# An ALiBi attention stage, rewritten as one pipeline over sequences

## The chip, the cores and the metric

The kernel runs on one core of a Trainium2 chip. The metric is the device time of one execution in microseconds. The profiled execution is one run of the same program, and its times are counted from the first instruction (the span's start).

## What is computed

A decoder of four layers runs over x, eight sequences of 128 positions and 256 features, in float32. Each layer has three sublayers, twelve stages in all. The change is in the first sublayer of the third layer, a causal self-attention with ALiBi (a bias that grows with distance, with a slope for each head), 16 heads of 16 features:

```python
qkv = jnp.einsum('bsd,de->bse', x, W_qkv)
q, k, v = jnp.split(qkv, 3, axis=-1)
q, k, v = (to_heads(q), to_heads(k), to_heads(v))
attn = jnp.einsum('bhqd,bhkd->bhqk', q, k) / math.sqrt(HEAD_DIM)
attn = attn + alibi_bias(seq_len, N_HEADS)[None] + causal_mask(seq_len)[None, None]
attn = jax.nn.softmax(attn, axis=-1)
y = jnp.einsum('bhqk,bhkd->bhqd', attn, v)
y = y.transpose(0, 2, 1, 3).reshape(bsz, seq_len, n_embd)
return jnp.einsum('bsd,de->bse', y, W_o)
...
x = x + _L2_attn_ref(_layernorm(x, axis=-1), L2_attn_W_qkv, L2_attn_W_o)
```

The slope of head h (from 1 to 16) is 2 to the power -8/h.

## The kernel before

Five queues run side by side: TensorE (PE), VectorE (DVE), ScalarE (ACT), GpSimd (POOL) and SyncE (SP), which starts the DMAs. Each runs its own instructions in the order in which they are written, and waits on semaphores for the others. There is no planner. The stages follow each other, and x, all eight sequences, stays in SBUF.

The stage of the change, L2a, is a loop `Fori(0, 4)` on each of the three engines, over pairs of sequences (suffixes 0 and 1, each with half of PSUM, `ps0` and `ps1`). For one sequence:

- VectorE normalises x (`bn_stats`, `bn_aggr`, `tensor_scalar`, L2815 to L2828, and for the next pair L2925 to L2945) with a ScalarE `Ln` and `Exp` for the inverse root. TensorE transposes the result, ScalarE copies it to SBUF (`unT0`, `unT1`).
- TensorE makes q and k, transposed, with eight matmuls (L4084 and L4091), and v with two (L4095, L4099).
- To separate heads of 16 features inside 128 partitions, VectorE multiplies k with the mask `mask16` into eight copies (`kM_0`, `kM_1`, L2832 to L2836, 128x1024 each, two a sequence). A matmul of 128 rows then gives the scores of four heads, 128x512, because seven eighths of k are zeros.
- For each group of four heads (four groups a sequence): VectorE adds the bias head by head out of PSUM, takes the row maxima, and multiplies them by -0.25. ScalarE takes the exponentials head by head, with the maximum as bias. TensorE transposes four 128x128 blocks, ScalarE copies them (`PT_0`), TensorE multiplies with v. v has a 17th column of ones, so that the sum of a row comes out with the product, VectorE takes the reciprocal of four sums and multiplies.
- TensorE transposes the result (`ao_0`), ScalarE copies it, TensorE applies the output weights (L4205, L4220), VectorE adds x (L2947, L2949).

```python
dve.scalar_tensor_tensor(S_0[:, 3, :], alibi[:, :], 1.0, ps0[:, 1, 384:512], ALU.mult, ALU.add)
...
dve.tensor_reduce(st0[:, 16:20], S_0[:, :, :], AX.X, ALU.max).then_inc(L2a_vector_done, 1)
...
dve.tensor_scalar(st0[:, 16:20], st0[:, 16:20], -0.25, None, ALU.mult).then_inc(L2a_vector_done, 1)
...
                for i in range(4):
                    last = act.activation(S_0[:, i, :], S_0[:, i, :], ACT.Exp, scale=0.25, bias=st0[:, 16 + i:17 + i])
```

`alibi` holds key position minus query position, and -1e30 where the key lies ahead of the query. GpSimd does nothing in the stage but one memset for a later stage (L1143), which waits for L2a. SP issues the weights of a later stage (L964 to L982) when L2a's last projection is done.

The stage behind it, L2x, starts with statistics of x (L2959, L2961), a ScalarE table load, and the scaling of its weights.

Two stages further on use shapes that matter here. The last one, L3f, has scores as eight matmuls of 32 rows and 256 columns (L4698, 16 records), outputs as matmuls of 32 weight columns (L4715), maxima and subtractions over 128x1024 (L3375, L3381). The one before it, L3x, takes a reciprocal of 128x256 (L3296).

## Time and profile before

| | us |
|---|---|
| median of 3 runs | 2380.74 (2378.89 to 2381.53) |
| the profiled execution | 2377.16 |
| its span, first to last instruction | 2375.4 |
| TensorE busy | 1984.6 (84%) |
| VectorE busy | 1531.1 (64%) |
| ScalarE busy | 1149.6 (48%) |
| GpSimd busy | 921.4 (39%) |

The busy times are sums over the whole program; which engine holds a stage up must be read from that stage. TensorE's granted clock over the whole span is 0.919 of its full 2.4 GHz. A float32 matmul shows as two records, a transpose as one.

### The profile page before, as it was taken

How to read it: one execution, taken by the hardware profiler on the slowest of the kernel's cores; microseconds unless marked ns; L12 is line 12 of the kernel's file. 1: busy time of each engine (PE TensorE's matmuls, PEld its weight loads, DVE VectorE, ACT ScalarE, POOL GpSimd, SP SyncE). 2: the span in 40 equal slices, each digit the busy share in tenths (PEclk: the TensorE clock that was granted, in tenths of full speed). 3: DMA queues.
4: the chain of work that ended last, by engine and by line, in shares of the span. 5: the costliest groups of instructions: out<-in, count | busy, mean ns of one | idle time of the engine just before them, and what ended most of it. 6: DMA issues, size and time to landing. Idle time of an engine off the chain costs nothing.

```text
span 2375.4 us, 32699 instructions
## 1 busy us (share of the span) xinstructions
PE 1984.6 (84%) x10924; PEld 1460.6 (61%) x10924; DVE 1531.1 (64%) x2892; ACT 1149.6 (48%) x2702; POOL 921.4 (39%) x651
## 2 busy tenths in 40 slices
PE   6677797786899886679999999967888879977999
PEld 5111185344799764467777777756777755544888
DVE  5798824557444575456666666548999967866443
ACT  4444323342232355655555555546666645644443
POOL 2699801210000000144444454439999950002221
PEclk9688897798899897789999999988999988998999
DMA  4111001002000502000000000000000010000000
GB/s 149 38 36 27 0 1 53 18 16 106 18 0 0 213 0 91 0 1 1 1 1 1 1 1 1 1 18 1 1 1 1 25 43 30 1 1 0 6 7 9
DMA packets 20858, 54.66 MB, mean 23 GB/s; under 512 B 8319, under 2 KB 13608, under 8 KB 18424
## 3 DMA queue, kind: packets, MB, share of 16 engines
q1 hardware_dynamic: 20728, 53.01, 6.6%
q8 instruction: 72, 1.18, 0.2%
q14 instruction: 58, 0.48, 0.1%
HBM read 44.61 MB, written 1.05 MB: 19 GB/s over the span
## 4 chain that ended last, share of the span: by engine, by line
PE 48%; DVE 20%; ACT 11%; issue 11%; POOL 9%; SPq 1%; DMA 0%; DVEq 0%; POOLq 0%; ACTq 0%
POOL sbuf L1193 4%; DVE sbuf L2237 3%; PE psum L4309 3%; PE psum L4251 3%; DVE sbuf L3001 2%; PE psum L3551 2%; POOL sbuf L1201 2%; ACT sbuf L1826 2%; PE psum L4299 2%; PE psum L4382 1%; PE psum L4735 1%; PE psum L4756 1%; PE psum L4742 1%; DVE sbuf L2993 1%; PE psum L4255 1%
## 5 line engine op out<-in xcount | busy, mean ns | idle before, releaser
L1193 POOL TENSOR_TENSOR sbuf<-sbuf 128x1035 f32<-128x1035 f32 x128 | 248.4, 1971 | 0.9 <-ACT sbuf L1894 0.9
L4382 PE MATMUL psum<-sbuf 128*128 128x128 f32 (+1 forms) x1024 | 144.4, 292 | 56.0 <-ACT sbuf L1903 39.6
L1903 ACT ACTIVATE sbuf<-sbuf 128x1001 f32<-128x1001 f32 (+1 forms) x128 | 141.6, 1139 | 97.9 <-DVE sbuf L3144 63.6
L4382 PEld LDWEIGHTS psum<-sbuf 128*128 128x128 f32 (+1 forms) x1024 | 126.3, 153 | 77.5 <-ACT sbuf L1903 55.9
L1155 POOL TENSOR_TENSOR sbuf<-sbuf 128x512 f32<-128x512 f32 x64 | 69.7, 1090 | 230.9 <-DVE sbuf L3018 230.9
L1082 POOL TENSOR_TENSOR sbuf<-sbuf 128x1024 f32<-128x1024 f32 x64 | 149.9, 2356 | 15.6 <-DVE sbuf L2237 14.9
L2237 DVE TENSOR_TENSOR_SCAN sbuf<-psum,sbuf 128x1024 f32<-128x1024 f32 x64 | 144.6, 2277 | 13.6 <-ACT psum L1314 6.9
L3499 PE MATMUL psum<-sbuf 96*128 96x512 bf16 x256 | 84.0, 439 | 75.1 <-DVE sbuf L2237 32.3
L4251 PE MATMUL psum<-sbuf 128*128 128x512 f32 x256 | 124.1, 608 | 17.4 <-DVE sbuf L2980 17.4
L3136 DVE SCALAR_TENSOR_TENSOR psum<-sbuf,psum 128x1024 f32<-128x1024 f32 (+1 forms) x96 | 122.3, 1274 | 12.8 <-PE psum L4372 5.4
L4309 PE MATMUL psum<-sbuf 128*128 128x256 f32 x512 | 125.5, 389 | 4.9 <-POOL sbuf L1163 4.9
L1314 ACT ACTIVATE psum<-psum,sbuf 128x1016 f32<-128x1016 f32 x64 | 68.9, 1081 | 125.1 <-PE psum L3499 125.1
L1826 ACT ACTIVATE sbuf<-psum,sbuf 128x128 f32<-128x128 f32 x256 | 90.6, 366 | 77.3 <-DVE sbuf L3012 77.3
L3144 DVE TENSOR_TENSOR sbuf<-psum,sbuf 128x1024 f32<-128x1024 f32 (+1 forms) x96 | 116.4, 1212 | 3.3
L1143 POOL MEMSET sbuf<- 128x720 f32 x1 | 0.7, 700 | 302.9 <-PE psum L4106 302.9
L3499 PEld LDWEIGHTS psum<-sbuf 96*128 96x128 bf16 x256 | 19.0, 104 | 152.8 <-DVE sbuf L2237 60.3
L4309 PEld LDWEIGHTS psum<-sbuf 128*128 128x128 f32 x512 | 99.6, 195 | 20.2 <-POOL sbuf L1163 6.1
L4299 PE MATMUL psum<-sbuf 128*128 128x256 f32 x256 | 73.3, 409 | 39.8 <-ACT sbuf L1833 39.8
L1161 POOL TENSOR_TENSOR sbuf<-sbuf 128x512 f32<-128x512 bf16 x64 | 74.4, 1162 | 68.6 <-DVE sbuf L3031 66.4
L3001 DVE TENSOR_REDUCE sbuf<-sbuf 128x6 f32<-128x768 f32 x64 | 60.8, 949 | 52.2 <-ACT sbuf L1796 52.2
L1163 POOL TENSOR_TENSOR sbuf<-sbuf 128x512 f32<-128x512 f32 x64 | 81.4, 1272 | 5.0
L3530 PE MATMUL psum<-sbuf 128*32 128x512 f32 x256 | 78.9, 748 | 3.5 <-POOL sbuf L1082 3.5
(1073 smaller groups left out, 5253.9 us busy)
## 6 DMA issues: line engine op xcount, KB each, us to landing
sbuf<-sbuf SPq DMA_DIRECT2D x42, 128.0 KB, 2.4
sbuf<-w_gu_d SPq DMA_DIRECT2D x1, 4096.0 KB, 13.6
sbuf<-w_p_d SPq DMA_DIRECT2D x1, 4096.0 KB, 25.3
sbuf<-w_qkv_d SPq DMA_DIRECT2D x3, 768.0 KB, 4.2
sbuf<-w_e_d SPq DMA_DIRECT2D x1, 2048.0 KB, 7.5
sbuf<-w_dn_d SPq DMA_DIRECT2D x1, 2048.0 KB, 16.6
sbuf<-w_q_d SPq DMA_DIRECT2D x1, 2048.0 KB, 7.4
sbuf<-w_qx_d SPq DMA_DIRECT2D x1, 2048.0 KB, 11.9
```

What stands on the lines that cost most here:

```text
L1082: pool.tensor_tensor(L0a_hc[i % 4][:, :], L0a_hs[i % 2][:, :], L0a_Cr[g % 4][:, :], ALU.mult).then_inc(hc_done, 1)
L1193: pool.tensor_tensor(P_r[g % 7][:, :, :], rows.unsqueeze(2).to_broadcast([128, 23, 45]), cols.unsqueeze(1).to_broadcast([128, 23, 45]), AL ...
L1826: last = act.activation(prob[:, h, :], L2x_s[:, h, :], ACT.Exp, bias=smax[:, h:h + 1], accum_out=esum[:, h:h + 1])
L1903: act.activation(Q_r[g % 6][:, 0:w], Q_r[g % 6][:, 0:w], ACT.Silu, scale=q8_p[n % 2][:, h:h + 1]).then_inc(silu_done, 1)
L2237: dve.tensor_tensor_scan(L0a_hs[i % 2][:, :], L0a_dAf[i % 2][:, :], L0a_us[i % 3][:, :], 0.0, ALU.mult, ALU.add).then_inc(scan_done, 1)
L3001: dve.tensor_reduce(ssum[:, :], sq[:, :, :], AX.X, ALU.add).then_inc(ss_done, 1)
L3136: dve.scalar_tensor_tensor(M[:, 0:w], Pf_r[g % 7][:, o:o + w], t8_p[n % 2][:, h, 7:8], zps[:, 0:w], ALU.is_ge, ALU.mult).then_inc(mask_don ...
L3144: dve.tensor_tensor(Q_r[g % 6][:, 0:w], Mps[:, 0:w], Pf_r[g % 7][:, o:o + w], ALU.mult).then_inc(prod_done, 1)
L4251: last = pe.matmul(L2x_q[:, :, :], xs[:, vq, c, :], wq[:, c, 512 * g:512 * g + 512], start=c == 0, stop=c == 1)
L4299: last = pe.matmul(L2x_o[:, 2 * h:2 * h + 2, :], v2_r[i % 3][:, h, :], pT2[:, 2 * h:2 * h + 2, :], start=True, stop=True)
L4309: last = pe.matmul(L2x_out[:, :], cat[:, h, :], w_p2[:, 4 * (i % 8) + h, :], start=i % 8 == 0 and h == 0, stop=i % 8 == 7 and h == 3)
L4382: last = pe.matmul(Gps[0:m, c, :], Q_r[g % 6][:, 128 * c:128 * c + m], ident[:, :], start=h == 0 and c % 4 == 0, stop=h == 7, skip_group_c ...
```

## The change

The three `Fori` loops of L2a are replaced by one pipeline over the eight sequences, written out, with its own small functions and the semaphores of the neighbouring stages.

- Scores: k is expanded by a mask of two (`L2a_mask2`) instead of eight, 128x512 a sequence. Four matmuls of 32 rows each, at partitions 0, 32, 64 and 96, take two heads each, twice: eight matmuls of 256 columns for all 16 heads.
- Bias: GpSimd fills a table of all slopes times `alibi`, -1e30 included, 16 blocks of 128x128, early in the kernel. VectorE adds it to the scores in two operations of 128x1024 (`L2a_bias`).
- Softmax: VectorE takes the maxima over 128x1024 and subtracts them itself (`L2a_sub`); ScalarE takes two exponentials of 128x1024 without bias.
- Outputs come transposed, with v as 32 weight columns (16 of them zeros); 16 more matmuls with `L2a_ones` give the row sums, repeated over the features, 128x256. VectorE takes the reciprocal of all 128x256 and multiplies. No transpose of the result is needed.
- GpSimd normalises x. The statistics of all sequences are taken at the stage's start.
- The waits of SP, of GpSimd's memset and of the next stage go to the new semaphores, and the starting numbers of later stages' semaphores change with them.

```diff
+            for a in range(2):
+                for h in range(8):
+                    head = h // 2 % 2 * 8 + 4 * a + h // 4 * 2 + h % 2
+                    last = pool.tensor_scalar(L2a_table[:, a, h, :], alibi[:, :], 4.0 * 2.0 ** (-8.0 / (head + 1)), None, ALU.mult)
+            last.then_inc(factor_done, 1)
...
+                pool.tensor_scalar(L2a_u[:, :], x[:, n, :], L2a_mv[:, n, 0:1], L2a_r[:, n:n + 1], ALU.subtract, ALU.mult).then_inc(u_done, 1)
...
+            def L2a_exp(n, a):
+                act.wait_ge(sub_done, L2a_start['sub'] + 2 * n + a + 1)
+                act.activation(L2a_P[a][:, :, :], L2a_P[a][:, :, :], ACT.Exp, scale=0.25).then_inc(exp_done, 1)
+
+            def L2a_pTc(n, a):
+                act.wait_ge(pT_done, L2a_start['pT'] + 2 * n + a + 1)
+                if n > 0:
+                    act.wait_ge(o_done, L2a_start['o'] + n)
+                act.activation(L2a_PT[a][:, :, :], L2a_pT[:, :, :], ACT.Copy).then_inc(pTc_done, 1)
...
+            for i in range(9):
+                if i > 0:
+                    L2a_pTc(i - 1, 1)
+                if i < 7:
+                    L2a_qTc(i + 1)
+                if i < 8:
+                    L2a_exp(i, 0)
+                if i < 7:
+                    L2a_vc(i + 1)
+                if i < 8:
+                    L2a_pTc(i, 0)
+                    L2a_exp(i, 1)
+                if i < 6:
+                    L2a_unTc(i + 2)
...
+            def L2a_keys(n):
+                dve.wait_ge(qTc_done, L2a_start['qTc'] + n + 1)
+                if n > 0:
+                    dve.wait_ge(score_done, L2a_start['score'] + n)
+                dve.tensor_tensor(L2a_kM[:, :, :, :], L2a_front[:, 256:512].rearrange('p (c s) -> p c s', c=2).unsqueeze(2).to_broadcast([128, 2, 2, 128]), L2a_mask2[:, None, :].unsqueeze(3).to_broadcast([128, 2, 2, 128]), ALU.mult).then_inc(kTc_done, 1)
+
+            def L2a_bias(n, a):
+                dve.wait_ge(score_done, L2a_start['score'] + n + 1)
+                if n > 0:
+                    dve.wait_ge(pT_done, L2a_start['pT'] + 2 * n + a - 1)
+                dve.tensor_tensor(L2a_P[a][:, :, :], L2a_S8[a][:, :, :], L2a_table[:, a, :, :], ALU.add).then_inc(prod_done, 1)
...
+                dve.tensor_reduce(L2a_mx[a][:, :], L2a_P[a][:, :, :], AX.X, ALU.max).then_inc(max_done, 1)
...
+                dve.tensor_tensor(L2a_P[a][:, :, :], L2a_P[a][:, :, :], L2a_mx[a][:, :].unsqueeze(2).to_broadcast([128, 8, 128]), ALU.subtract).then_inc(sub_done, 1)
+
+            def L2a_scale(n):
+                dve.wait_ge(o_done, L2a_start['o'] + n + 1)
+                dve.reciprocal(L2a_rec[:, :, :], L2a_sums[:, :, :]).then_inc(recip_done, 1)
+                dve.wait_ge(recip_done, L2a_start['recip'] + n + 1)
+                if n > 0:
+                    dve.wait_ge(proj_done, L2a_start['proj'] + n)
+                dve.tensor_tensor(L2a_aoT[:, :, :], L2a_oT[:, :, :], L2a_rec[:, :, :], ALU.mult).then_inc(norm_done, 1)
+
+            def L2a_resid(n):
+                dve.wait_ge(proj_done, L2a_start['proj'] + n + 1)
+                dve.tensor_tensor(x[:, n, :], L2a_out[:, :], x[:, n, :], ALU.add).then_inc(resid_done, 1)
...
+            for i in range(9):
+                if i < 8:
+                    L2a_bias(i, 0)
+                    L2a_max(i, 0)
+                    L2a_sub(i, 0)
+                    L2a_bias(i, 1)
+                if i < 7:
+                    L2a_keys(i + 1)
+                if i < 8:
+                    L2a_max(i, 1)
+                    L2a_sub(i, 1)
+                if i > 0:
+                    L2a_scale(i - 1)
+                    L2a_resid(i - 1)
...
+            def L2a_scores(n):
+                pe.wait_ge(kTc_done, L2a_start['kTc'] + n + 1)
+                if n > 0:
+                    pe.wait_ge(prod_done, L2a_start['prod'] + 2 * n)
+                for c in range(2):
+                    for r in range(4):
+                        last = pe.matmul(L2a_S[:, r, c, :, :], L2a_qT[32 * r:32 * r + 32, c, :], L2a_kM[32 * r:32 * r + 32, c, :, :], start=True, stop=True)
+                last.then_inc(score_done, 1)
...
+                            pe.matmul(L2a_oT[32 * r:32 * r + 32, c, :], L2a_v[n % 2][:, 4 * c + r, 32 * e:32 * e + 32], L2a_PT[r // 2][:, 4 * (r % 2) + 2 * c + e, :], start=e == 0, stop=e == 1)
...
+                            last = pe.matmul(L2a_sums[32 * r:32 * r + 32, c, :], L2a_ones[:, 32 * e:32 * e + 32], L2a_PT[r // 2][:, 4 * (r % 2) + 2 * c + e, :], start=e == 0, stop=e == 1)
+                last.then_inc(o_done, 1)
+
+            def L2a_project(n):
+                pe.wait_ge(norm_done, L2a_start['norm'] + n + 1)
+                for c in range(2):
+                    last = pe.matmul(L2a_out[:, :], L2a_aoT[:, c, :], w_o2[:, c, :], start=c == 0, stop=c == 1)
+                last.then_inc(proj_done, 1)
...
+            for i in range(9):
+                if i < 8:
+                    L2a_scores(i)
+                if i > 0:
+                    L2a_pTr(i - 1, 1)
+                if i < 7:
+                    L2a_qk(i + 1)
+                if i > 0:
+                    L2a_pv(i - 1)
+                if i < 7:
+                    L2a_value(i + 1)
+                if i < 8:
+                    L2a_pTr(i, 0)
+                if i < 6:
+                    L2a_uTr(i + 2)
+                if i > 0:
+                    L2a_project(i - 1)
```

Not shown are `L2a_uTr`, `L2a_qk`, `L2a_value` (the same matmuls as before, one sequence at a time), `L2a_pTr` (eight transposes), `L2a_unTc`, `L2a_qTc`, `L2a_vc` (ScalarE's copies), the statistics, and the memsets for v and ones.

## Rows read from the trace of the kernel before

**Rows 1.** Busy time by engine: the stage, and one loop pass (two sequences).

```profile
core 0: us, PE busy (x) PEld busy (x) DVE busy (x) ACT busy (x) POOL busy (x), PEclk, DMA share, GB/s
788.37:932.68 144.31, 126.87 (x676) 94.86 (x676) 93.24 (x312) 73.98 (x214) 0.70 (x1) 0.88 0.17 72
861.70:896.00 34.30, 30.83 (x168) 22.84 (x168) 22.84 (x76) 18.15 (x52) 0.00 (x0) 0.90 0.00 0
```

**Rows 2.** Timeline at the stage's end: start, us, engine, line, idle before.

```profile
932.26 0.42 DVE L2949 TENSOR_TENSOR sbuf<-psum,sbuf 128x256 f32 x1 [2.33 <-PE psum L4220]
932.76 1.28 ACT L1835 ACT_TABLE_LOAD   x1
932.78 0.42 DVE L2959 BATCH_NORM_STATS2 sbuf<-sbuf 128x6 f32<-128x256 f32 x1
933.24 0.18 DVE L2961 BATCH_NORM_AGGREGATE sbuf<-sbuf 128x2 f32<-128x6 f32 x1
```

**Rows 3.** List of waits in the stage: us in total, times, longest us.

```profile
POOL sbuf L1143 <- PE psum L4106: 302.9, 1, 302.9
...
DVE sbuf L2949 <- PE psum L4220: 9.7, 4, 2.5
DVE sbuf L2939 <- PE psum L4200: 9.6, 4, 2.7
```

**Rows 4.** VectorE groups by shape, whole program: busy us, mean ns of one.

```profile
L2227 DVE TENSOR_TENSOR sbuf<-psum,sbuf 128x1024 f32<-128x1024 f32 x42 | 51.4, 1224 | 20.6 <-PE psum L3499 17.4
L3387 DVE TENSOR_REDUCE sbuf<-sbuf 128x8 f32<-128x1024 f32 x16 | 19.2, 1198 | 11.7 <-ACT sbuf L2110 11.7
L3296 DVE RECIPROCAL sbuf<-sbuf 128x256 f32<-128x256 f32 x4 | 7.0, 1750 | 0.0
L3369 DVE TENSOR_TENSOR sbuf<-psum,sbuf 128x512 f32<-128x512 f32 x8 | 5.5, 690 | 9.8 <-ACT sbuf L2098 9.7
L3221 DVE RECIPROCAL sbuf<-psum 128x16 f32<-128x16 f32 x16 | 3.9, 244 | 4.1 <-PE psum L4518 4.1
```

**Rows 5.** Timeline, two runs of the same VectorE product, the second beside GpSimd.

```profile
382.55 1.22 DVE L2368 TENSOR_TENSOR sbuf<-sbuf 128x1024 f32<-128x1024 f32 x1
...
392.05 0.72 POOL L1104 TENSOR_TENSOR sbuf<-sbuf 128x256 f32<-128x256 f32 x1 [13.44 <-DVE sbuf L2392]
392.09 1.76 DVE L2368 TENSOR_TENSOR sbuf<-sbuf 128x1024 f32<-128x1024 f32 x1
```

**Rows 6.** Timeline of the last stage: transposes, outputs, row-tiled scores, maxima.

```profile
2243.64 2.03 PE L4704 MATMUL psum<-sbuf 128*128 128x128 f32 x16
...
2247.32 1.08 PE L4715 MATMUL psum<-sbuf 128*32 128x128 f32 x32
...
2249.30 0.74 PEld L4698 LDWEIGHTS psum<-sbuf 32*128 32x128 f32 x16 [0.42 <-issue]
...
2250.52 1.23 DVE L3375 TENSOR_REDUCE sbuf<-psum 128x8 f32<-128x1024 f32 x1 [2.66 <-PE psum L4698]
```

**Rows 7.** Timeline of the stage before it: a projection and its residual add.

```profile
2139.24 1.13 PE L4651 MATMUL psum<-sbuf 128*128 128x256 f32 x4 [0.47 <-ACT sbuf L2067]
...
2140.10 0.24 PEld L4656 LDWEIGHTS psum<-sbuf 128*128 128x128 f32 x2
...
2140.52 0.42 DVE L3347 TENSOR_TENSOR sbuf<-psum,sbuf 128x256 f32 x1 [0.47 <-PE psum L4651]
```

**Rows 8.** ScalarE and GpSimd groups by shape, whole program.

```profile
L2116 ACT ACTIVATE sbuf<-psum 128x1024 f32<-128x1024 f32 x16 | 16.1, 1025 | 19.5 <-PE psum L4704 19.4
...
L1242 POOL TENSOR_SCALAR sbuf<-sbuf 128x256 f32<-128x256 f32 x8 | 9.8, 1220 | 6.0 <-DVE sbuf L3363 6.0
```

**Rows 9.** Busy time by engine and granted clock in three other stretches.

```profile
892.00:896.00 4.00, 3.97 (x14) 3.10 (x14) 1.48 (x5) 0.41 (x2) 0.00 (x0) 0.50 0.00 0
...
1760.00:1762.00 2.00, 0.15 (x2) 0.00 (x0) 2.00 (x4) 1.94 (x4) 2.00 (x2) 1.00 0.01 4
...
1600.00:1900.00 300.00, 247.18 (x1677) 214.17 (x1676) 282.10 (x414) 199.81 (x272) 288.37 (x149) 0.95 0.02 6
```

**Rows 10.** Timeline, the stage's first projection of q and k.

```profile
792.08 3.53 PE L4084 MATMUL psum<-sbuf 128*128 128x128 f32 x16 [0.86 <-ACT sbuf L1667]
```

More of the change, by code:

```diff
@@ L963, in _ @@
             sp.wait_ge(L2a_w_loaded, 32)
[L964 removed]
+            sp.wait_ge(proj_done, L2a_start['proj'] + 8)
             sp.dma_start(w_u2[:, :, :], w_u2_d).then_inc(L2f_w_loaded, 16)
@@ L2954, in _ @@
+            dve.wait_ge(resid_done, L2a_start['resid'] + 8)
             dve.memset(eps2[:, :], 1e-10)
@@ L4232, in L2x_uTr @@
+            pe.wait_ge(resid_done, L2a_start['resid'] + 8)
             def L2x_uTr(n):
```

544 lines of the change are left out of this document (143 added, 401 removed).

## The prediction

> **What bounds the kernel now.** The table by stretches comes first. The ALiBi attention stage runs from 788.37 us to 932.68 us of the span (its last add starts at 932.26 and takes 0.42) [rows 1, 2]: 144.3 us of 2375.4. The reader is to see there that no engine is full. TensorE's records fill 127 of 144 us, VectorE 95, ScalarE 93, GpSimd 0.7. One pass over two sequences (861.70 to 896.00, 34.3 us) shows the same, 17.2 us a sequence [rows 1]. So the stage is bound by the order of hand-overs. The list of waits shows which: VectorE waits for TensorE at the end of every pass (9.7 us before the residual add, 9.6 us before the last reciprocal), and GpSimd has slept 302.9 us when its one instruction here starts [rows 3]. Nothing overlaps the stage from outside: the engines that open it wait for the last stage's x, and the next stage's statistics start 0.1 us after the last add [rows 2]. A microsecond taken out of the stage is therefore one off the total, and the question is only how long the new stage is.
>
> **What goes.** Per sequence 16 bias operations of 128x128, four maxima of 128x512, two key expansions of 128x1024, 16 small exponentials and the small reciprocals and products go; wide operations take their place, six of 128x1024 on VectorE and four on ScalarE. Per sequence VectorE now has 95/8 = 11.9 us of records, ScalarE 9.2, TensorE 15.9 [rows 1]. The new ones are priced below.
>
> **The loop of the new stage.** I follow the chain that sets its period. VectorE does, for sequence i and score halves 0 and 1: `bias(i,0)`, `max(i,0)`, `sub(i,0)`, `bias(i,1)`, `keys(i+1)`, `max(i,1)`, `sub(i,1)`, then `scale(i-1)` (reciprocal, product), `resid(i-1)`. TensorE's order puts `scores(i+1)` right behind `project(i-1)`, which waits for that product, and `bias(i+1,0)` waits for `scores(i+1)`. That closes the loop. Prices, all of the same operation and shape:
> - two bias adds, 128x1024, PSUM and SBUF in: 2 x 1.22 (L2227) [rows 4]
> - two maxima over 128x1024 in SBUF: 2 x 1.20 (L3387) [rows 4]
> - two subtractions, both inputs in SBUF: 2 x 1.22, as the undisturbed one (at 382.55) [rows 5]
> - keys, 128x512 out of PSUM: 0.69 (L3369) [rows 4]
> - the reciprocal. It used to be 4 numbers a row; now the sums come as full 128x256. Such a reciprocal takes 1.75 us (L3296) [rows 4], four times the product behind it. That row reads SBUF, the new one PSUM; 16 elements from PSUM already take 0.24 (L3221) [rows 4], so PSUM is no way around it. I take 1.75.
> - the product, 128x256: 0.42, as the residual add of the same shape [rows 2].
>
> Sum 2.44 + 2.40 + 2.44 + 0.69 + 1.75 + 0.42 = 10.1; the few hundredths by which neighbours overlap or hand over I leave out, as they go both ways. Then project and scores: 0.05 to start, 0.86 until TensorE is free of the four projection records (2139.24 to 2140.10 [rows 7]), and 1.22 from the first row-tiled score matmul to VectorE's start on the result (2249.30 to 2250.52 [rows 6]; the last stage issues the very same 16 records). Period: 10.14 + 0.05 + 0.86 + 1.22 = 12.3 us a sequence against 17.2. `resid` lies in that gap: 1.28 from project's start to the add [rows 7] plus 0.42 is 1.7 of 2.13, so it costs nothing; with the gap gone it would cost its 0.42.
>
> Is another engine longer than 12.3? TensorE, at full clock: scores 1.0, 16 transposes 2.03 [rows 6], qk about 1.9 and value 0.9 as now, output and sums 64 records of 128x32 weights, where 32 take 1.08 [rows 6], so 1.9, input transposes 0.2, project 0.9: 8.8. ScalarE: two exponentials and two copies of 128x1024 at 1.03 [rows 8], three or four small copies, 5.4. GpSimd: one normalisation of 1.22 [rows 8]. So VectorE plus the project and scores pair decides. Within the period the transposes and copies have slack: `pTr(i-1,1)` runs behind scores, pv ends about 4.5 into the period and the reciprocal wants it at 7.8; keys want `qTc` at 4.8 and get it at 3.0.
>
> **Start, first turn, tail.** Start: statistics, logarithm and exponential as now; the normalisation moves to GpSimd, which takes 1.22 for one [rows 8] where VectorE takes some 0.4, but only one sequence is waited for and not two, so the first qk comes 0.3 later than today's 792.08. It runs at half clock, 3.53 us [rows 10]. Then copy 0.4, keys 0.7, value 1.1, its copy 0.5, transposes and scores 1.5: first bias at 12.0 us into the stage. From the first bias to the second 8.7 (VectorE 5.5 to the end of `keys(1)`, then value, transposes, scores). Six periods: 73.8. Tail from `bias(7,0)`: 9.4 to the end of `scale(6)`, project 0.9, eight transposes 1.0, copy 1.05, output and sums 1.95, reciprocal and product 2.25, project to add 1.33, add 0.42: 18.4. Sum 12.0 + 8.7 + 73.8 + 18.4 = 112.9, that is 31.4 less than 144.3. The table build (16 GpSimd operations of 128x128) and the norms cost nothing: they lie in the 302.9 us in which GpSimd waits [rows 3]; if that cover were gone, the table's some 10 us would be due (0.6 each, half of the 1.22 of rows 8, an estimate). Zeroing v and ones lies under the logarithm and the first qk.
>
> **Behind the stage.** ScalarE's table load of 1.28 us begins after its last copy, and ends 0.6 after VectorE has the next stage's statistics (933.24 + 0.18 against 934.04 [rows 2]). ScalarE's last copy will now be 5 us before the end, so this 0.6 goes. SP's loads for the feed-forward stage wait for the last projection, now as before; their queue has nothing nearer behind it. The keys memset on GpSimd, 0.7 us [rows 1], moves to the same point; GpSimd's next work, on the quantised input, is behind statistics, transposes and copies of the next stage. The other semaphore offsets cost nothing.
>
> **The clock.** At 892 to 896 us, behind waits and narrow matmuls, the granted clock is 0.50, which is 1.2 GHz [rows 9]. Against that, a bare wait of two microseconds inside dense work (1760 to 1762, TensorE 0.15 busy) stays at 1.00, 2.4 GHz [rows 9]. The new period has such a wait (from the input transposes at 7.4 to project at 10.2) between about 7 us of dense work and TensorE some 75% busy. The nearest rows with that pattern are the 300 us from 1600, 82% busy at clock 0.95 [rows 9]: 10% of the time at half speed. Only TensorE work on the chain is hurt, 8 x 2.1 plus some 10 us at start and end, 27 us: 3 us. Bounds: 0, and 1.9 a period where project and scores always fall in it, 15 us.
>
> **Two prices put against the Trainium skill.** A GpSimd addition under a two-input VectorE product stretched it from 1.22 to 1.76 [rows 5]. GpSimd's normalisation could do that to `sub`. It starts when the input transposes are out, 7.5 to 8.9 in the period, just as `sub(i,1)` ends (7.8) and the reciprocal, one input, in PSUM, begins. I take 0; bound 0.55 x 16 = 8.8. The Trainium skill (GPSIMD Engine Reference, section 8, Key points) has it as a rule: GpSimd shares its SBUF interfaces with VectorE and contends with instructions that have two SBUF inputs. By that rule each overlap is paid, and the sum would lose up to those 8.8; the trace agrees with the rule, and what is open is only whether the two meet.
>
> Before the row-tiled scores the weight loads idle 0.42 for issue [rows 6]. I count 0 extra, since the 1.22 includes what follows; bound 0.42 x 8 = 3.4. The Trainium skill (TensorEngine Tiling (Array Packing), Key Properties) says that a change of tiling mode drains TensorE; by it I would put the 3.4 in, and no row here separates a drain from issue.
>
> **Sum.** 31.4 + 0.6 - 3.0 = 29.0 us. The profiled execution took 2377.16 us (span 2375.4 plus 1.8 around it), so its like would take 2348.2. The three runs' median is 3.6 higher, 2380.74, and the forecast is for a median: 2352.
>
> **Rivals.**
> - The clock takes project and scores every time. For it: the wait sits right ahead of them, and the 0.50 of rows 9. Against: 1760 to 1762. Period 14.2; 32.0 - 15 = 17 gained: 2364.
> - The subtractions collide with GpSimd. One a sequence 4.4, both 8.8, on top of the 3: 2356 to 2361. For it: rows 5. Against: the order in time above.
> - The reciprocal costs as little as other passes, 0.42. Period 11.0, 8 x 1.33 = 10.6 more gained: 2341. Against: both rows of it.
> - The other side: TensorE at 1.2 GHz throughout. Its 8.8 us a sequence become 17.6, longer than VectorE's chain, and TensorE is the bound. 12.0 + 3 at the start, 8.7 + 3, six of 17.6, 18.4 + 5 in the tail: 155.7 against 144.3, so 2391. It decides from a period of (144.9 - 39.1)/6 = 17.6 at an unchanged start and tail, 15.8 at slower ones. Against: the stage of before is not less patchy and has 0.88.
>
> That the stage is hidden anyway is excluded by the waits at both its ends.
>
> **Chances and range.** Forecast 0.60, clock 0.16, collision 0.10, cheap reciprocal 0.05, half clock throughout 0.04; 0.05 for what no row shows (the loop written out eight times must be fetched), mostly still faster. The range goes from the cheap reciprocal, 2341, to the clock rival with 3.4 more for issue, 2367; the forecast's own is 2348 to 2357. Faster by over 0.2% (4.8 us, about what a measurement of this kernel can tell from no change) 0.94, within 0.02, slower 0.04.
>
> **What would show it.** Right: `bias(i,0)` to `bias(i+1,0)` 12.3 us; the 128x256 reciprocal 1.75 and a gap of 2.1 us on VectorE, with only the residual add in it, before each first bias; subtractions at 1.22; clock about 0.95. Wrong: a period of 14 with 0.7 in the clock; 1.7 us subtractions; VectorE waiting in the middle of a period, for `keys` or the reciprocal, which would mean slack I have not got; or a reciprocal of another size.

## The result, and the profile after

The changed kernel's median is 2356.06 us (four runs, 2352.28 to 2358.96) beside 2380.65 for the kernel before, taken again in the same group of runs: ratio 0.9894, 95% interval 0.988 to 0.9909. That is 24.6 us less; the forecast was 2352 and 29.0. The profiled execution took 2352.28 us, span 2350.4.

The table by stretches, of the changed kernel: the whole stage, the ends of the three turns that are longer than the others, a stretch of the stage's tail, and last a turn's boundary that runs at full clock (column PEclk).

```profile
core 0: us, PE busy (x) PEld busy (x) DVE busy (x) ACT busy (x) POOL busy (x), PEclk, DMA share, GB/s
787.30:906.18 118.88, 84.36 (x976) 68.75 (x976) 86.37 (x102) 43.48 (x69) 10.10 (x9) 0.90 0.21 89
832.00:834.00 2.00, 2.00 (x8) 1.17 (x11) 0.20 (x1) 0.00 (x0) 0.00 (x0) 0.50 0.00 0
858.00:862.00 4.00, 4.00 (x25) 2.82 (x26) 1.32 (x2) 0.00 (x0) 0.00 (x0) 0.61 0.00 0
872.00:874.00 2.00, 2.00 (x19) 1.09 (x18) 0.42 (x1) 0.00 (x0) 0.00 (x0) 0.64 0.00 0
896.00:900.00 4.00, 3.18 (x12) 2.45 (x12) 0.42 (x1) 0.78 (x1) 0.00 (x0) 0.57 0.02 4
844.00:848.00 4.00, 2.43 (x23) 1.69 (x24) 2.06 (x4) 1.34 (x3) 0.68 (x1) 1.00 0.00 0
```

The stage takes 118.9 us instead of 144.3 [rows 1]. VectorE's 86.4 now exceed TensorE's 84.4. VectorE's groups by shape, in the stage:

```profile
L2819 DVE TENSOR_TENSOR sbuf<-sbuf 128x1024 f32<-128x1024 f32 x16 | 19.6, 1224 | 0.6
L2809 DVE TENSOR_TENSOR sbuf<-psum,sbuf 128x1024 f32<-128x1024 f32 x16 | 19.5, 1220 | 12.0 <-PE psum L4001 12.0
L2815 DVE TENSOR_REDUCE sbuf<-sbuf 128x8 f32<-128x1024 f32 x16 | 19.4, 1215 | 0.3
L2823 DVE RECIPROCAL sbuf<-psum 128x256 f32<-128x256 f32 x8 | 14.0, 1750 | 4.4 <-PE psum L4025 4.4
L2803 DVE TENSOR_TENSOR sbuf<-psum,sbuf 128x512 f32<-128x512 f32 x8 | 5.4, 681 | 3.9 <-ACT sbuf L1693 3.9
```

In this order: subtraction, bias, maxima, reciprocal, keys. All have the prices of [rows 4], the subtraction that of the undisturbed product of [rows 5], and the reciprocal takes 1750 ns out of PSUM too. Ahead of these VectorE idles before the bias (12.0 us, for the scores) and once each before the first keys and the last reciprocal, nowhere inside a turn.

The timeline of one turn's boundary, undisturbed (start, us, engine, line, idle before):

```profile
845.09 0.42 DVE L2827 TENSOR_TENSOR sbuf<-psum,sbuf 128x256 f32<-128x256 f32 x1
845.57 1.13 PE L4031 MATMUL psum<-sbuf 128*128 128x256 f32 x4 [2.29 <-DVE sbuf L2827]
846.63 1.15 PE L4001 MATMUL psum<-sbuf 32*128 32x256 f32 x16
846.74 0.42 DVE L2831 TENSOR_TENSOR sbuf<-psum,sbuf 128x256 f32<-128x256 f32 x1 [1.22 <-PE psum L4031]
847.85 1.22 DVE L2809 TENSOR_TENSOR sbuf<-psum,sbuf 128x1024 f32<-128x1024 f32 x1 [0.68 <-PE psum L4001]
```

and one turn earlier, where the clock falls to 0.50:

```profile
829.42 1.75 DVE L2823 RECIPROCAL sbuf<-psum 128x256 f32<-128x256 f32 x1
829.57 1.22 POOL L1159 TENSOR_SCALAR sbuf<-sbuf 128x256 f32<-128x256 f32 x1 [11.09 <-PE psum L3979]
831.21 0.42 DVE L2827 TENSOR_TENSOR sbuf<-psum,sbuf 128x256 f32<-128x256 f32 x1
831.68 2.08 PE L4031 MATMUL psum<-sbuf 128*128 128x256 f32 x4 [2.29 <-DVE sbuf L2827]
833.69 1.77 PE L4001 MATMUL psum<-sbuf 32*128 32x256 f32 x16
833.80 0.42 DVE L2831 TENSOR_TENSOR sbuf<-psum,sbuf 128x256 f32<-128x256 f32 x1 [2.17 <-PE psum L4031]
835.54 1.22 DVE L2809 TENSOR_TENSOR sbuf<-psum,sbuf 128x1024 f32<-128x1024 f32 x1 [1.32 <-PE psum L4001]
```

The chain is the predicted one in both: product (L2827), project (L4031), scores (L4001), first bias (L2809), with the residual add (L2831) in the gap, and GpSimd's normalisation (L1159) under the reciprocal. Project and scores together take 2.28 us at full clock, and 3.86 where most of them runs at half. The eight first biases start at 800.45, 809.34, 821.65, 835.54, 847.85, 861.10, 874.03 and 886.34, so the six turns are 12.31, 13.89, 12.31, 13.25, 12.93 and 12.31 us. Three are undisturbed. At the ends of the other three the clock is 0.50, 0.61 and 0.64 in the stretches of the table. In the first of them project and scores are both longer (2.08 and 1.77 us instead of 1.13 and 1.15), in the other two only the scores (2.09 and 1.78).

The stage's end, to set beside [rows 2]:

```profile
904.59 1.13 PE L4031 MATMUL psum<-sbuf 128*128 128x256 f32 x4 [2.34 <-DVE sbuf L2827]
905.76 0.42 DVE L2831 TENSOR_TENSOR sbuf<-psum,sbuf 128x256 f32<-128x256 f32 x1 [1.22 <-PE psum L4031]
906.22 0.42 DVE L2867 BATCH_NORM_STATS2 sbuf<-sbuf 128x6 f32<-128x256 f32 x1
906.89 0.29 ACT L1758 ACTIVATE sbuf<-sbuf 128x1 f32<-128x1 f32 x1 [5.35 <-DVE sbuf L2869]
```

ScalarE starts the next stage 0.71 us after the last add; before, it was free at 934.04, 1.36 after the add, because of its table load. These 0.65 us are the 0.6 of the forecast.

### The profile page after: what moved, and what is told of

It is laid out like the page before. It is cut to its first block, busy times and chain, and to the rows that moved or that the text cites. A ratio compares the mean times of both kernels' runs of the same rounds, so it can differ in the third digit from the quotient of the medians.

```text
span 2350.4 us, 32604 instructions
## 1 busy us (share of the span) xinstructions
PE 1939.9 (83%) x11224; PEld 1432.9 (61%) x11224; DVE 1524.9 (65%) x2682; ACT 1116.8 (48%) x2556; POOL 939.0 (40%) x675
## 4 chain that ended last, share of the span: by engine, by line
PE 45%; DVE 22%; issue 11%; ACT 10%; POOL 10%; SPq 1%; DMA 0%; DVEq 0%; POOLq 0%; ACTq 0%
POOL sbuf L1219 5%; DVE sbuf L2217 3%; PE psum L4136 3%; PE psum L4078 3%; DVE sbuf L2909 3%; POOL sbuf L1227 2%; PE psum L3459 2%; PE psum L4126 2%; ACT sbuf L1806 2%; DVE psum L3044 1%; PE psum L4562 1%; POOL sbuf L1091 1%; PE psum L4583 1%; PE psum L4569 1%; DVE sbuf L2901 1%
## 5 line engine op out<-in xcount | busy, mean ns | idle before, releaser
L1091 POOL TENSOR_TENSOR sbuf<-sbuf 128x1024 f32<-128x1024 f32 x64 | 149.8, 2354 | 16.5 <-DVE sbuf L2217 16.5
L2217 DVE TENSOR_TENSOR_SCAN sbuf<-psum,sbuf 128x1024 f32<-128x1024 f32 x64 | 144.8, 2278 | 12.3 <-ACT psum L1340 7.2
L1159 POOL TENSOR_SCALAR sbuf<-sbuf 128x256 f32<-128x256 f32 x8 | 9.8, 1220 | 235.0 <-ACT sbuf L1683 176.7
L1274 POOL TENSOR_TENSOR sbuf<-sbuf 128x1024 f32<-128x1024 f32 x16 | 30.3, 1914 | 129.6 <-DVE sbuf L3299 129.6
```

What stands on the lines that cost most here:

```text
L1091: pool.tensor_tensor(L0a_hc[i % 4][:, :], L0a_hs[i % 2][:, :], L0a_Cr[g % 4][:, :], ALU.mult).then_inc(hc_done, 1)
L2217: dve.tensor_tensor_scan(L0a_hs[i % 2][:, :], L0a_dAf[i % 2][:, :], L0a_us[i % 3][:, :], 0.0, ALU.mult, ALU.add).then_inc(scan_done, 1)
```

## The experiments

Each was timed in turns with the kernel before. Groups of runs differ by a few us, so the third column is the difference to the kernel before in the same group. The stage is counted from the first statistics (start of `bn_stats` for sequence 0) to the end of the last residual add, in the profile; a turn is from `bias(i,0)` to `bias(i+1,0)`, the six from sequence 1 to 7 (all of them where they differ, otherwise the repeating one).

| | median us | to before | ratio, 95% interval | stage us | turn us |
|---|---|---|---|---|---|
| before | 2374.92 to 2380.65 | 0 | | 144.3 | 17.2 |
| changed kernel | 2356.06 | -24.6 | 0.9894, 0.988 to 0.9909 | 118.9 | 12.31 to 13.89 |
| the same again | 2355.32 | -22.7 | 0.9909, 0.9892 to 0.9925 | 118.9 | 12.31 to 13.90 |
| scores ahead of project | 2343.41 | -33.5 | 0.9863, 0.9848 to 0.9878 | 108.8 | 10.28, first 12.04 |
| reciprocal on ScalarE | 2342.92 | -33.9 | 0.9856, 0.9841 to 0.9871 | 105.3 | 10.71 |
| subtraction on ScalarE | 2343.48 | -33.4 | 0.9857, 0.9842 to 0.9872 | 106.2 | 10.22, first 11.89 |
| gap filled | 2358.85 | -18.0 | 0.992, 0.9907 to 0.9934 | 123.9 | 12.31, last 13.61 |
| gap filled, later | 2352.41 | -25.6 | 0.9894, 0.9877 to 0.991 | 118.4 | 12.31 |
| work added on GpSimd | 2363.4 (one run) | | | 126.5 | 12.31 to 15.99 |
| narrow bias | 2362.29 | -12.6 | 0.9947, 0.993 to 0.9964 | 126.6 | 13.21, one 14.77 |
| back half not overlapped | 2425.29 | +50.4 | 1.0209, 1.0191 to 1.0228 | 187.5 | 19.07 to 23.25 |
| scores ahead and reciprocal on ScalarE | 2333.07 | -44.9 | 0.9807, 0.9779 to 0.9834 | 102.9 | 9.98, first 11.62 |
| q and k first | 2339.88 | -35.0 | 0.9842, 0.9813 to 0.987 | 106.1 | 10.54 |
| transposes first | 2329.69 | -47.4 | 0.9801, 0.9785 to 0.9817 | 91.9 | 8.79, one 9.07 |

### Scores ahead of project

```diff
@@ TensorE, in each turn
                 if i < 7:
                     L2a_value(i + 1)
+                    L2a_scores(i + 1)
@@ VectorE, in each turn
                     L2a_bias(i, 0)
+                if i > 1:
+                    L2a_resid(i - 2)
```

> The changed kernel with one thing moved: TensorE issues scores(i+1) right behind value(i+1), ahead of project(i-1), and VectorE takes the residual add of sequence i-1 behind the first bias of sequence i+1. Theory (VectorE's chain plus the gap of project and scores sets the period): the gap of 2.13 us ahead of each first bias goes and the residual add's 0.42 becomes due, so the period falls from 12.31 to 10.14 + 0.42 = 10.56 us, the periods no longer depend on the clock, and the time falls by 11 to 14 us, to about 2343. Rival (TensorE, with some 9 us of work and waits inside the period, or ScalarE's order is nearly as long as VectorE): another wait takes the gap's place, in the middle of VectorE's period, and the period stays above 11.5, a gain under 6 us.

The turn falls to 10.28 us, and the stage by 10.1. From the first bias of sequence 1 on, the six turns take 13.6 us less (63.4 instead of 77.0), but up to there this profile takes 3.0 us more, with TensorE at half clock (its first value matmuls 2.07 us instead of 1.13), and the tail 0.5 more. The first of the six turns is 12.04 us: behind 1.8 us of idle TensorE's transposes take 1.87 instead of 1.09, so the turns had not become independent of the clock, as the expectation has it. By the times the edit is worth 8.9 to 10.8 us beside the changed kernel's two groups, under the 11 to 14 expected. The timeline of this kernel at a turn's boundary:

```profile
841.60 0.42 DVE L2827 TENSOR_TENSOR sbuf<-psum,sbuf 128x256 f32<-128x256 f32 x1
841.95 1.22 DVE L2809 TENSOR_TENSOR sbuf<-psum,sbuf 128x1024 f32<-128x1024 f32 x1
842.08 1.13 PE L4034 MATMUL psum<-sbuf 128*128 128x256 f32 x4 [1.04 <-DVE sbuf L2827]
843.25 0.42 DVE L2831 TENSOR_TENSOR sbuf<-psum,sbuf 128x256 f32<-128x256 f32 x1
```

No VectorE line has an idle time: the bias starts while the product ends. The theory holds: VectorE's chain and the gap of project and scores set the period. The turn is 0.28 under the 10.56 expected: VectorE operations that don't need each other's result start some 0.08 us before the one ahead has ended (the bias here, 0.07), which the sum left out.

### The reciprocal on ScalarE

```diff
-                dve.reciprocal(L2a_rec[:, :, :], L2a_sums[:, :, :]).then_inc(recip_done, 1)
...
+                act.activation(L2a_rec[:, :, :], L2a_sums[:, :, :], ACT.Ln).then_inc(L2a_ln_done, 1)
+                act.wait_ge(L2a_ln_done, n + 1)
+                act.activation(L2a_rec[:, :, :], L2a_rec[:, :, :], ACT.Exp, scale=-1.0).then_inc(recip_done, 1)
```

> The changed kernel with VectorE's reciprocal of 128x256 replaced by a logarithm and an exponential of the negative on ScalarE, issued behind the copy of v. Theory (the reciprocal's 1.75 us lie whole on the chain): the period falls by 1.75 to 10.56 us, the tail by 1.75 less two hand-overs to ScalarE, in all 12 to 14 us, time about 2343. Rival (the reciprocal fills a wait for output and sums, which on TensorE's side end only shortly before it): VectorE then waits for the sums, and less than half of it, under 7 us, comes back.

The turn falls by 1.60 to 10.71, the stage by 13.6: the 1.75 us lie on the chain but for 0.15. Two activations of 128x256 take its place, 0.39 and 0.42 us long, on an engine that has room. All six turns are equal, with project 1.13 and scores 1.15 in each. By the times it is 9.3 to 11.2 us, short of the 12 to 14 expected.

### The subtraction on ScalarE

```diff
-                dve.tensor_tensor(L2a_P[a][:, :, :], L2a_P[a][:, :, :], L2a_mx[a][:, :].unsqueeze(2).to_broadcast([128, 8, 128]), ALU.subtract).then_inc(sub_done, 1)
+                dve.tensor_scalar(L2a_nm[a][:, :], L2a_mx[a][:, :], -0.25, None, ALU.mult).then_inc(sub_done, 1)
...
-                act.activation(L2a_P[a][:, :, :], L2a_P[a][:, :, :], ACT.Exp, scale=0.25).then_inc(exp_done, 1)
+                for h in range(8):
+                    last = act.activation(L2a_P[a][:, h, :], L2a_P[a][:, h, :], ACT.Exp, scale=0.25, bias=L2a_nm[a][:, h:h + 1])
```

> The changed kernel with the subtraction given back to ScalarE, as before the change: VectorE multiplies the eight maxima by -0.25 (128x8) in place of the 128x1024 subtraction, and ScalarE takes eight exponentials of 128x128 with the maximum as bias in place of one of 128x1024. Theory (VectorE's chain sets the period): VectorE's 2.44 us of subtractions become about 0.2, the period falls from 12.31 to about 10.1 us, and ScalarE, 5.4 us a sequence before, comes to about 8.5 and stays under it; the time falls by 14 to 18 us, to about 2340. Rival (the subtraction on VectorE is what lets ScalarE keep up): the second half's exponentials, 2.6 us instead of 1.05, reach the transposes too late, VectorE waits for TensorE inside the period, and the period stays at 11.5 to 13 us.

The turn falls to 10.22, as the theory says, and the stage by 12.6 us, less than the 14 to 18 that the time was to fall by; by the times it is 8.8 to 10.7. The first of its turns is 11.89, and the tail (20.4 us from 874.55 to 894.96) is no shorter than the changed kernel's 19.8. Two lines of this kernel's timeline show the trade:

```profile
846.40 0.17 DVE L2824 TENSOR_SCALAR sbuf<-sbuf 128x8 f32<-128x8 f32 x1
...
847.50 2.44 ACT L1707 ACTIVATE sbuf<-sbuf 128x128 f32<-128x128 f32 x8
```

The part of the change that gives VectorE the subtractions therefore costs about 2.1 us a turn by itself. ScalarE could have kept them.

### Filling TensorE's gap

```diff
@@ input transposes; first form: from the third sequence on, second: from the fourth on
-                for c in range(2):
+                for c in [0, 1] * (8 if n > 2 else 1):
                     last = pe.transpose(L2a_front[:, 128 * c:128 * c + 128], L2a_u[:, 128 * c:128 * c + 128], ident[:, :])
@@ second form only, ahead of project
+                if i in (6, 7):
+                    pe.wait_ge(vc_done, L2a_start['vc'] + 8)
+                    for c in range(16):
+                        pe.transpose(L2a_front[:, 128 * (c % 2):128 * (c % 2) + 128], ident[:, :], ident[:, :])
```

> The changed kernel with the two input transposes of each sequence from the third on repeated eight times in place (the same result, 14 more transposes of 128x128, about 2 us), so that TensorE's idle 2.3 to 2.5 us ahead of project shrink to some 0.5 us. Theory (the idle stretch lowers the granted clock, and project and scores then run at 1.2 GHz): all six periods come to 12.3 us, project 1.13 and scores about 1.1 us in each, the time falls by 2 to 4 us, to about 2353, and the runs scatter less. Rival (the clock follows something else than this stretch): half-clock projections stay as often as before, and the time does not change, 2356, or rises a little.

Of this kernel's turns the five with filler are 12.31 us each (814.03 to 875.59), and the one without, the last, is 13.61. But from the first bias to the second it takes 12.10 instead of 8.89: the filler of sequence 2 stood ahead of `scores(1)`. The time did not fall, and the expectation for the time failed: the gain over the kernel before is 18.0 us instead of 22.7 to 24.6. Outside the filled turns this profile meets more half clock than the changed kernel's: 14.5 us to the first bias instead of 13.2, and a tail of 22.1 instead of 19.8, with project at 2.08. (The second form, below, has 10.56 there without filler, so half of the 3.2 is the filler's and half the clock's at the start.)

> The changed kernel once more, nothing altered. It gives a second profile of it and its time beside the same runs of the kernel before as the experiments. Theory (what exceeds 12.31 us in a period comes from a granted clock that differs from run to run): the undisturbed periods are 12.31 us again, the long ones stand at other places or in another number, 0 to 6 of six, and nothing but TensorE's project and scores is longer in them. Rival (the long periods belong to the program, say to the fetching of the written-out loop): the same periods are long by the same amounts.

The expected scatter is not there, and the sign that was given for the rival is: the second profile of the changed kernel has turns of 12.31, 13.90, 12.31, 13.26, 12.94 and 12.31 us, the pattern of the first to 0.01. The long turns belong to the program. They are no fetching of code, the rival's example, all the same: what is longer in them are TensorE's own records, at a granted clock of 0.50. Its line for the second turn:

```profile
830.60 2.07 PE L4031 MATMUL psum<-sbuf 128*128 128x256 f32 x4 [2.29 <-DVE sbuf L2827]
```

> As the first filling experiment, but the input transposes are repeated only from the fourth sequence on, where TensorE has time for them, and the last two turns, which have no input transposes, get 16 transposes of the identity at the same place. The first one paid 3.2 us for its filler in the first turn, where the first bias of sequence 1 waits for it, and its seventh turn, without filler, was 13.61 us long, while the five filled ones were 12.31. Theory (the idle stretch ahead of project lowers the clock): start to second bias as in the unfilled kernel, every filled turn 12.31 us, and 2 to 4 us less than the unfilled kernel in the same group of runs. Rival (the fills were beside the point and the clock of this kernel wanders): filled turns of 13 us appear, and no gain.

All six turns are 12.31 us. The project of the second turn, in this kernel's timeline:

```profile
833.26 1.91 PE L3979 MATMUL psum<-sbuf 128*128 128x128 f32 x16
835.93 1.13 PE L4031 MATMUL psum<-sbuf 128*128 128x256 f32 x4 [0.76 <-DVE sbuf L2827]
```

With 0.76 us of idle ahead of it project runs at full clock; with 2.29 it ran at half in one turn and at full in another. The one turn of the first form without filler, with 2.51 us of idle, has its drop too. So in these runs the long idle stretch is a condition for the drop and not enough for it. The filler makes TensorE busier as well as the idle stretch shorter, and these two are not told apart. The loop takes 73.9 us instead of 77.0, as expected. But the start took 25.0 us to the second bias where the changed kernel took 22.0, on code that does not differ: value(0) ran at half clock (2.08 us instead of 1.13), and later groups too. The stage is only 0.5 us shorter, and the gain of some 3 us against the same group (-25.6 and -22.7) is within what the spread of these runs (2346.51 to 2354.01, 2351.99 to 2358.81) allows by chance.

### Work added on GpSimd

```diff
+                if 1 < n < 6:
+                    for k in range(4):
...
+                        if n % 2:
+                            pool.tensor_tensor(L2a_scr[:, :], L2a_table[:, 0, :, :].rearrange('p h s -> p (h s)'), L2a_table[:, 1, :, :].rearrange('p h s -> p (h s)'), ALU.add).then_inc(L2a_scr_done, 1)
+                        else:
+                            pool.tensor_scalar(L2a_scr[:, :], L2a_table[:, 0, :, :].rearrange('p h s -> p (h s)'), 0.5, None, ALU.mult).then_inc(L2a_scr_done, 1)
```

> The changed kernel with work added on GpSimd behind the normalisation of sequences 2 to 5: four passes over 128x1024 of the slope table into a scratch area, one input times a constant for sequences 2 and 4, the sum of two inputs for 3 and 5. They start when the product is due and lie under the next turn's bias, maxima and subtraction. Theory (the new stage's subtractions stay at 1.22 us only because GpSimd is idle beside them): under the additions of two inputs the subtraction takes about 1.76 us, the bias and the maxima, which read one SBUF operand at most, stay at 1.22, and each covered subtraction adds 0.5 us to its period; under the one-input passes nothing or less than 0.2. Rival (the stretched product of the kernel before was special to its stage): all subtractions stay at 1.22 and the period at 12.3.

VectorE's timeline of this kernel in one turn under additions of two inputs (a GpSimd record of four runs from 812.84 for 11.39 us):

```profile
812.95 1.22 DVE L2826 TENSOR_REDUCE sbuf<-sbuf 128x8 f32<-128x1024 f32 x1
814.20 2.09 DVE L2830 TENSOR_TENSOR sbuf<-sbuf 128x1024 f32<-128x1024 f32 x1
816.21 1.21 DVE L2820 TENSOR_TENSOR sbuf<-psum,sbuf 128x1024 f32<-128x1024 f32 x1
817.95 1.20 DVE L2826 TENSOR_REDUCE sbuf<-sbuf 128x8 f32<-128x1024 f32 x1
819.18 2.83 DVE L2830 TENSOR_TENSOR sbuf<-sbuf 128x1024 f32<-128x1024 f32 x1
```

Bias (L2820) and maxima (L2826) keep their 1.2 us; the subtraction (L2830), the only one with both inputs in SBUF, goes to 2.09 and 2.83. A third one under such additions takes 1.53. Four lie under the one-input passes. Two of them take 1.79 and 1.94, against the expectation of nothing or under 0.2, and the other two keep 1.22 and 1.23. The timeline tells why in the single passes:

```profile
834.13 2.77 POOL L1170 TENSOR_SCALAR sbuf<-sbuf 128x1024 f32<-128x1024 f32 x1
834.30 1.94 DVE L2830 TENSOR_TENSOR sbuf<-sbuf 128x1024 f32<-128x1024 f32 x1
845.38 3.22 POOL L1168 TENSOR_TENSOR sbuf<-sbuf 128x1024 f32<-128x1024 f32 x1
```

The two stretched ones start 0.2 and 0.3 us behind the start of a pass and end 2.1 us behind it; the two others start 1.9 and 2.2 us into a pass. Under the additions each of the three ends 1.1 us after the pass that it began in, and the next pass takes 3.2 us instead of 2.4 (as the one at 845.38). So whichever comes second waits, GpSimd too.

The Trainium skill (SBUF — State Buffer, SBUF: two separate sides) says that VectorE with two SBUF inputs and GpSimd reading SBUF exclude each other, and that the one that starts first holds the ports for its whole instruction. The additions agree with that. The one-input passes agree that one input on GpSimd's side is enough, but not on the whole instruction: both stretched subtractions end 0.7 us before the pass of 2.8 us does, as far as GpSimd's rough spans can tell. The turns of this kernel are longer than the subtractions explain (15.99 with scores and project at half clock, 2.09 and 1.39, and the next normalisations late), so their length prices nothing by itself.

### Narrow bias

```diff
-                dve.tensor_tensor(L2a_P[a][:, :, :], L2a_S8[a][:, :, :], L2a_table[:, a, :, :], ALU.add).then_inc(prod_done, 1)
+                for h in range(8):
...
+                    last = dve.scalar_tensor_tensor(L2a_P[a][:, h, :], alibi[:, :], 4.0 * 2.0 ** (-8.0 / (head + 1)), L2a_S8[a][:, h, :], ALU.mult, ALU.add)
```

> The changed kernel with the slope table unused: the bias of each half is added head by head, eight scalar_tensor_tensor of 128x128 each, as in the kernel before (0.28 us each there), in place of one addition of 128x1024 (1.22). Theory (the table shortens the chain only by the fixed part of seven small operations): neighbours overlap by some hundredths, eight take 1.7 to 2.2, so 1.0 to 2.0 us more a period, 13.3 to 14.3, and the time rises by 8 to 16 us. Rival (the narrow operations stream as the wide one does): under 0.3 us a period, no change in the time.

The undisturbed turn is 13.21, 0.90 us longer, just below the theory's 1.0. The eight run into each other:

```profile
852.59 1.67 DVE L2811 SCALAR_TENSOR_TENSOR sbuf<-sbuf,psum 128x128 f32<-128x128 f32 x8 [0.68 <-PE psum L4004]
```

1.67 against 1.22. Against the kernel before it stands 12.6 us better where the changed one stands 22.7 to 24.6: the table is worth 10 to 12 us by the times, 7.7 in the stage.

### The back half not overlapped

```diff
@@ TensorE, in each turn
                     L2a_pTr(i, 0)
                 if i < 6:
                     L2a_uTr(i + 2)
-                if i > 0:
-                    L2a_project(i - 1)
+                if i < 8:
+                    L2a_pTr(i, 1)
+                    L2a_pv(i)
+                    L2a_project(i)
@@ ScalarE takes L2a_pTc(i, 1) at the turn's end, VectorE scale(i) and resid(i)
```

> The changed kernel with every new operation kept, but the overlap of sequences taken out of its back half: transposes, outputs, reciprocal, product, project and residual add of sequence i all come before the scores of sequence i+1 (q, k and v of the next sequence are still made ahead). Theory (most of the gain is the order, not the wider operations): the period is the whole chain of one sequence. From the rows of the changed kernel: 7.85 from the first bias to the end of the second subtraction, then wait for the copy before it, exponential 1.05, transposes 1.05, copy 1.0, output and sums 2.0, reciprocal and product 2.2, project and scores 2.2, with hand-overs about 17.9 us, about the 17.2 of the kernel before; the time is 2385 to 2395, all of the gain gone or more. Rival (the fewer and wider operations carry the gain by themselves): the period stays under 15 us and the time under 2370.

The gain is gone and more: the stage takes 187.5 us, longer than the 144.3 of before. The direction is the theory's, the size is not: 20.64 us in the turns from 846.05 and 866.69, not 17.9. The stage in this kernel's table by stretches:

```profile
789.93:977.40 187.47, 113.91 (x976) 88.73 (x976) 87.03 (x102) 43.71 (x69) 10.12 (x9) 0.73 0.14 57
```

and the timeline of the turn from 866.69:

```profile
872.21 2.07 PE L3992 MATMUL psum<-sbuf 128*128 128x256 f32 x4 [2.78 <-DVE sbuf L2803]
873.32 1.23 DVE L2819 TENSOR_TENSOR sbuf<-sbuf 128x1024 f32<-128x1024 f32 x1
876.59 1.05 ACT L1705 ACTIVATE sbuf<-sbuf 128x1024 f32<-128x1024 f32 x1
881.92 1.76 DVE L2823 RECIPROCAL sbuf<-psum 128x256 f32<-128x256 f32 x1 [7.37 <-PE psum L4025]
885.25 2.03 PE L4001 MATMUL psum<-sbuf 32*128 32x256 f32 x16
```

Ahead of the reciprocal VectorE is idle for 7.4 us, the mean clock of the stage is 0.73 instead of 0.90, and value at half clock (2.07) delays the first transposes and their copy, so that the second exponential starts 2.0 us after its subtraction ended. The scores at half clock (2.03 instead of 1.15) make up another 0.9 of the 2.7 us above the theory. What the same order would cost at full clock was not run.

### Both, and in three orders

> Scores ahead of project and the reciprocal on ScalarE together. VectorE's chain, 10.28 us a turn with the scores ahead, loses 1.75 more and comes to 8.5; TensorE's work for a sequence, the records of the last trace summed, is about 9.0 to 9.5 with the changes of matmul kind. Theory (then TensorE is the bound): a period of 9.2 to 9.8 us, TensorE without a wait of over 0.5 us in it, and 5 to 9 us less than with the scores ahead alone. Rival (the two gains add, since TensorE's overheads overlap): a period of 8.5 and 12 us less.

9.98 us a turn: longer than the 9.2 to 9.8 of the theory, and not the 8.5 of the rival. TensorE is busy 18.02 of the 19.97 us from 833.19, and waits 0.97 for the second exponential in each turn, where the theory allowed no wait of over 0.5: it is not yet the bound. The four times lie in two pairs, 2328.4 and 2328.5 beside 2337.6 and 2339.9, and the profile is of one of the slower pair.

> The kernel with the scores ahead of project and the reciprocal on ScalarE had a period of 9.98 us, with waits in a ring: TensorE waits 1.4 us for the second exponential, which ScalarE issues behind the copy of the first half, q and k of the next sequence are queued behind those transposes, and the keys behind them. Here q and k are issued ahead of the second half's transposes, their copy ahead of the copy of those, and the copy of the normalised input ahead of the second exponential. Theory (the ring sets 9.98): the wait of TensorE shrinks, the period falls to 9.1 to 9.5 us, the time by 3 to 6 us. Rival (TensorE's own work of some 9.5 us with its 0.33 us gaps at each change of kind sets it): 9.7 to 10 us, no change.

A miss. The turn grows to 10.54: with q and k ahead, the outputs stand right behind the copy of their own transposes, and TensorE waits 1.1 us there instead. The edit moved three things at once (q and k, their copy, and the second exponential behind the copy of the input), and this wait is what the trace shows of them.

```diff
@@ TensorE: the first half's transposes up to behind the outputs, project ahead of the input transposes
+                if i < 8:
+                    L2a_pTr(i, 0)
                 if i < 7:
-                    L2a_value(i + 1)
                     L2a_scores(i + 1)
-                if i < 8:
-                    L2a_pTr(i, 0)
-                if i < 6:
-                    L2a_uTr(i + 2)
+                    L2a_value(i + 1)
                 if i > 0:
                     L2a_project(i - 1)
+                if i < 6:
+                    L2a_uTr(i + 2)
@@ ScalarE: L2a_recip(i - 1), L2a_pTc(i, 0), L2a_exp(i, 1) ahead of L2a_vc(i + 1)
```

> Scores ahead of project and the reciprocal on ScalarE, with another order in each turn: TensorE takes the first half's transposes of sequence i right behind the outputs of sequence i-1, then scores(i+1), value(i+1), project(i-1) and the input transposes; ScalarE takes the reciprocal and the first half's copy and second exponential ahead of the copy of v. The last reordering made the period longer, 10.54 against 9.98 us, since it put the outputs behind the copy of their own transposes. Theory (in the 9.98 us ring the first bias of a sequence waits for the first half's transposes of the one before, which stood behind the scores): both come about 0.7 us earlier, and the period falls towards TensorE's own sum, 8.95 us by the starts of its groups in that trace: 9.1 to 9.6 us and 3 to 6 us less than with the order of 9.98. Rival (the copy of v, now later, holds up the input transposes and with them the next q and k): 10 us or more.

Two turns of this last order in the table by stretches:

```profile
836.85:854.43 17.58, 17.58 (x246) 15.32 (x245) 16.66 (x20) 11.95 (x21) 2.44 (x2) 1.00 0.01 2
```

8.79 us a turn, under both the theory's range and its 8.95. TensorE is busy for all 17.58 us, VectorE for 16.66, and the clock is 1.00. TensorE is the bound now. At 2329.69 this is the best version, 47.4 us under the kernel before, about twice the gain of the change. Beside the order of 9.98 us a turn the profiled stage is 11.0 us shorter, but the medians only 3.4 (2.5 against the kernel before), because two of that version's four runs were as fast as these. No profile shows where those two runs gained.

## Why the prediction came out as it did

- **The bound of before, and that the stage is exposed**: right. The stage lost 25.4 us, and the total 24.6.
- **The loop**: right. The undisturbed turn is 12.31 against 12.3, and both ends of that number were tested: with the gap taken away the turn is 10.28, with the reciprocal away 10.71, with the subtractions away 10.22. That it agrees to 0.01 is partly luck, for inside it two small errors cancel: VectorE's part is 9.97 instead of 10.14 (835.54 to 845.51), and project holds TensorE 1.06 instead of 0.86 until the scores start. The 0.20 a turn, 1.6 us in all, lie inside the bound of 3.4 that stood for the change of matmul kind. Without such a change the next group starts 0.97 us after value's first record (827.17 to 828.14), so 0.09 of it is all that these rows give to the change of kind, far less than the 0.42 a turn that the Trainium skill's drain (TensorEngine Tiling (Array Packing), Key Properties) was given. TensorE's own sum, 8.8 us a sequence, was right too: the last version, where TensorE is the bound, takes 8.79.
- **The reciprocal of 1.75 us from PSUM**: right (1750 ns, eight times), and the cheap-reciprocal rival is out. It was the most useful row of the forecast: four times the price of the product of the same shape.
- **No collision with GpSimd**: right. The normalisation runs under the reciprocal (829.57 against 829.42), and the subtractions are at 1224 ns. The rival's mechanism is real: with GpSimd busy beside them five of seven took 1.5 to 2.8 us.
- **The clock**: the right mechanism, mis-sized. The forecast gave the clock 3.0 us, 10% of the 27 us of TensorE work on the chain. Measured at half clock: 1.2 us in the start (input transposes 0.66 and scores 2.09, instead of 0.38 and 1.15), 3.1 in three of the six turns (77.0 against 73.9), 1.3 in the tail (project 1.57, transposes 1.91 instead of 1.13 and 1.09), 5.6 in all. The stage came out at 118.9 against 112.9 + 3.0: the 3.0 us too many are this term within 0.4. (Two of the sum's terms are also added up loosely: the start's parts give 11.7 and not 12.0, the tail's 18.3 and not 18.4.) The step that was mis-sized is "the nearest rows with that pattern are the 300 us from 1600": they have a mean clock of 0.95, but in the new stage the drops fall just on the work behind the idle stretch, which is the chain's. The clock rival, which takes every turn, is out as well: three of six.
- **Behind the stage**: 0.65 us for the 0.6.
- **The table build**: hidden, as said. GpSimd's first normalisation had still waited 176.7 us; from 600 us to the stage it is busy 10.1 us instead of 1.4, so the table costs it 8.7 us, of the 10 estimated.

Stage and hand-over give 26.1 us, the medians 24.6 in one group and 22.7 in the other. What lies outside the stage has unchanged instructions but for the table, and differs from profile to profile: the stage's first statistics start between 784.35 and 791.05 us over the fourteen profiles, and what follows the stage lasts from 1437.8 to 1448.1. Whether a part of the 1.5 to 3.4 us is a cost of the change stays open; the profiles cannot tell it from that.

Also open: why three turns of the changed kernel keep the full clock behind the same 2.29 us of idle. It is the same in both profiles of the kernel, so it belongs to the program, but no experiment here separated what in it decides.

## What to carry to other kernels

Close the loop on paper: name the chain from an instruction in one turn to the same in the next, with the in-order queues as part of it, and price it from rows of equal shape; here that gave each part of the period to 0.2 us and named the edits that would shorten it. Then move work off the chain before making it faster: issuing the scores before the project that need not precede them was worth 10 us of stage. With the reciprocal on ScalarE besides, one more order of TensorE's and ScalarE's groups took another 11 us off the profiled stage (102.9 to 91.9, 3 us in the medians), and another plausible one added 3. A wait of TensorE on the critical chain can cost twice, since the work right behind it is what ran at the lower clock, here in three turns of six.

## What the runs showed of the hardware

- What the granted clock does behind an idle stretch of 2.3 us was no chance of the run here: two profiles of the same kernel drop in the same three turns of six, to 0.01 us. With 0.8 us of idle, none of six drops.
- At the stage's start it differs between profiles: from the first statistics to the first bias it takes 13.15 us in four profiles and 14.5 in the nine others of the new stage, on instructions that do not differ; value(0) is 1.13 us in the one kind and 2.08 in the other. Both profiles of the changed kernel are of the first kind and every other kernel has one profile, so chance and program are not told apart.
- A subtraction of 128x1024 with both inputs in SBUF goes from 1.22 to 1.8 or 1.9 us when it starts within 0.3 us of the start of a one-input GpSimd pass, and keeps 1.22 when it starts 1.9 us or more into one. Beside two-input passes it takes 1.5 to 2.8 and ends 1.1 us after the pass, and the pass behind it grows from 2.4 to 3.2. Bias and maxima beside them keep their 1.2.
- Eight VectorE operations of 128x128 in a row, 0.28 us each alone, take 1.67 together: 0.45 more than one of 128x1024.
